# Moments and scales of y for thirteen batches made in the first layer, each kept in a place of its own

## The chip, the cores and the metric

The kernel runs on one core of a Trainium2 chip. The time is device microseconds of one execution. The core has five engines that run their own instruction lists in order and meet through semaphores: TensorE (PE, matrix products), VectorE (DVE), ScalarE (ACT), GpSimd (POOL) and SyncE (SP, which here issues DMA transfers).

## What is computed

`x` is 16 batches of 512 nodes by 128 features, `adj` a 512 by 512 matrix. There are two residual layers, cut here to what matters:

```
h = relu(layernorm(x))
x = x + L0(h)      # eight Euler steps of a graph diffusion
h = relu(layernorm(x))
x = x + L1(h)      # see below

def L1(h):         # softmax attention with 4 heads of 32
    lam_max = eigvalsh(L)[-1]
    L_norm = 2.0 * L / lam_max - I
    z = relu(layernorm((L_norm @ h) @ Wc + bc) * g1 + be1)
    x1 = z + h
    o = masked_attention(x1 @ Wq, x1 @ Wk, x1 @ Wv) @ Wo + bo
    x2 = layernorm(x1 + o) * g2 + be2
    m = gelu(x2 @ W1 + b1) @ W2 + b2
    return layernorm(x2 + m) * g3 + be3
```

The change is about the second `relu(layernorm(x))`. The sum x + L0(h) is called `y` in the kernel; its layer norm needs a mean and a variance for each of the 512 nodes of a batch.

## The kernel before

All data of the 16 batches stay on the chip: `y` holds them as 128 partitions by 16 x 512. A batch is four tiles of 128 nodes.

The program is two blocks, `layer0` and `layer1`. At the end of a block all five engines wait for each other (the rows call it by L598 for the first block), and only then does the second block start.

**First block.** It runs over pairs of batches, `pair(p)` on each engine, p = 0 to 8; a pair enters at p and leaves at p + 1, so that p = 8 only finishes batches 14 and 15. TensorE makes node powers (`first_power`, L843), feature products (`feature_products`, L880) and the products that join them (`pair_product`, L851). VectorE splits results into a high and a low part (`T_lo`, L1263; `Y1_lo`, L1292), adds up the feature products (`C_out`, L1273 to L1276) and adds the last products to y in two halves (`y_out`, L1301). It makes the moments of x for the next batches (`x_moments`). GpSimd turns these into scales for the first layer norm (`scales`, L656 to L666) and puts x and bias into y (`x_and_bias`, L672), which `C_out` waits for. `pair(5)` and `pair(6)` also hold steps of the power iteration for lam_max and the first steps of the second layer (`early`).

**Second block.** Its loop is `round_(r, s, half)`, r = 1 to 18. In a round one batch is attended to, in 16 units `u`: TensorE makes scores (L1882), VectorE masks them (L2062), ScalarE makes exponentials (L2004), TensorE turns them (L1896), ScalarE or VectorE copies them (L1987, L2049), and TensorE multiplies by the values (L1916). Beside it the next batch is convolved (L1954), standardised (`z_out`, `z_moments`, `z_standard`, `norm_z`) and projected, and the one before leaves. The order within a round is a table of numbers by hand (`AT_X1` to `AT_Z2_STD`).

**Moments and scales of y.** `y_moments` is a wait, four statistics instructions (L305), a wait, and four that aggregate them into `mv_a` (L311), on VectorE. `h_scales` is four small operations on GpSimd (L228, L230, L238, L241): variance plus epsilon, its inverse root `rstd_a`, mean times root, and its negative `shift_a`. `normalise` (L250, ScalarE) makes h from y with them. There is one `mv_a`, and two places of `rstd_a` and `shift_a` used in turn; the waits on `scales` and `h_ready` guard them. Batches 0 and 1 are done in pair 5 of the first block, on VectorE around the feature products (`early(p, "y0")`, `early(p, "y1")`), on GpSimd between `x_and_bias(10)` and `scales(12)`. Batch 2 is done in pair 7. Batch r + 2, for 3 to 15, is done in round r of the second block: `y_moments` at unit 9 on VectorE, `h_scales` on GpSimd ahead of `add_bo`.

## Time and profile before

| | |
|---|---|
| three runs, us | 867.37, 867.99, 868.82 |
| median | 867.99 |
| profiled execution, us | 868.01 |
| its span, us | 866.2 |
| PE busy | 818.8 us, 95% |
| DVE busy | 646.5 us, 75% |
| ACT busy | 530.5 us, 61% |
| POOL busy | 310.4 us, 36% |
| first block, from the span's start | to about 395.9 us |

The span is what the profiler saw of the execution; 1.8 us of it lie outside. Shares are over the whole span, which joins two stages: in the first block DVE and ACT are about half busy, in the second both are 80 to 90% busy and more. An engine's idle time is shown in brackets behind the instruction that ended it, with the releaser, as inferred from semaphores. TensorE's clock is given as a share of 2.4 GHz, and is 1.00 or 0.50.

### The profile page before, as it was taken

Reading aid. Unit: us, or ns where it says so; the run is one execution under the profiler, and the core shown is the slowest. Engines: PE = TensorE matmul, PEld = TensorE weight load, DVE = VectorE, ACT = ScalarE, POOL = GpSimd, SP = SyncE. Lnnn points to the kernel's source line nnn. Section 1 sums busy time; section 2 is a strip of 40 time slices with the busy share of each in tenths; the row PEclk is TensorE's granted clock in tenths of the full one; section 3 lists DMA queues with packets and bytes.
Section 4 is the critical chain, followed back from the end, with each engine's and each line's share of the span. In section 5 each row is a group of like instructions: output and inputs, shape, how many; then the busy total and the mean of one; then the engine's idle time right before and its main releaser. Section 6 shows DMA issues by size and latency. Waiting matters only on the chain.

```text
span 866.2 us, 18914 instructions
## 1 busy us (share of the span) xinstructions
PE 818.8 (95%) x6609; PEld 690.4 (80%) x6609; DVE 646.5 (75%) x2146; ACT 530.5 (61%) x1223; POOL 310.4 (36%) x406
## 2 busy tenths in 40 slices
PE   6999999999999999998999999999999999999992
PEld 5778989898989888976777777777777777778982
DVE  5956464645477656536899999999999998987998
ACT  4434243434322422325988888898888888887884
POOL 2011121212122415300445545555554545432654
PEclk9999999999999999998999999999999999999997
DMA  6000010101010100312434455423344444322243
GB/s 133 1 13 13 13 37 13 37 14 37 13 37 13 37 25 26 101 46 76 119 94 108 133 136 135 134 94 96 96 124 135 135 136 133 103 49 63 82 139 97
DMA packets 57514, 65.59 MB, mean 76 GB/s; under 512 B 5574, under 2 KB 32844, under 8 KB 57420
## 3 DMA queue, kind: packets, MB, share of 16 engines
q1 hardware_dynamic: 57120, 64.25, 26.6%
q8 instruction: 53, 0.87, 0.4%
q14 instruction: 41, 0.34, 0.1%
q10 hardware_dynamic: 300, 0.13, 0.1%
HBM read 39.59 MB, written 24.77 MB: 74 GB/s over the span
## 4 chain that ended last, share of the span: by engine, by line
PE 21%; DVE 12%; issue 8%; POOL 8%; ACT 3%; DMA 1%; DVEq 0%; SPq 0%; POOLq 0%
PE bank L1896 6%; PE bank L1954 4%; PE bank L1916 4%; PE bank L1882 3%; DVE prob L2062 2%; PE bank L381 2%; POOL z_norm L353 2%; POOL z_gain L349 2%; POOL x_bo L1834 2%; DVE stats L1666 2%; ACT prob L2004 2%; POOL rstd_b L230 2%; PE bank L385 1%; DVE prob L1661 1%; DVE z L2101 1%
## 5 line engine op out<-in xcount | busy, mean ns | idle before, releaser
L2004 ACT ACTIVATE prob<-prob,low 128x512 f32<-128x512 f32 x256 | 183.7, 718 | 28.2 <-DVE low L2062 25.8
L2062 DVE CUSTOM_DVE_ANT_0 prob<-bank,mask 128x512 f32<-128x512 f32 x256 | 171.0, 682 | 8.5 <-PE bank L1882 6.3
L1896 PE MATMUL bank<-ident,prob 128*128 128x128 f32 x1024 | 158.3, 277 | 1.4 <-ACT probT L1987 1.0
L1896 PEld LDWEIGHTS bank<-ident,prob 128*128 128x128 f32 x1024 | 120.8, 141 | 42.1 <-issue 30.6
L1882 PE MATMUL bank<-k_stack,q_stack 96*128 96x512 f32 x256 | 124.1, 485 | 8.6 <-DVE low L2062 7.3
L1987 ACT ACTIVATE probT<-bank 128x512 f32<-128x512 f32 x176 | 103.1, 586 | 22.9 <-PE bank L1896 21.4
L880 PE MATMUL bank<-B_hi,halves 128*128 128x384 f32 x384 | 106.7, 341 | 3.0 <-DVE C L1276 1.6
L851 PE MATMUL bank<-halves,P3T_hi 128*128 128x256 f32 x512 | 93.9, 285 | 0.9 <-DVE halves L1292 0.5
L851 PEld LDWEIGHTS bank<-halves,P3T_hi 128*128 128x128 f32 x512 | 80.5, 191 | 4.4 <-DVE halves L1292 1.3
L880 PEld LDWEIGHTS bank<-B_hi,halves 128*128 128x128 f32 x384 | 70.6, 189 | 6.4 <-DVE halves L1263 2.7
L851 PE MATMUL bank<-halves,P3T_lo 128*128 128x256 f32 x256 | 72.4, 283 | 0.0
L656 POOL TENSOR_SCALAR var_eps<-mv 128x4 f32<-128x4 f32 x16 | 3.6, 226 | 190.0 <-DVE mv L1216 190.0
L1916 PE MATMUL bank<-probT,v 128*32 128x128 f32 x2048 | 69.2, 276 | 0.0
L2049 DVE COPY probT<-bank 128x512 f32<-128x512 f32 x80 | 55.0, 687 | 16.1 <-PE bank L1896 16.0
L880 PE MATMUL bank<-B_lo,halves 128*128 128x384 f32 x192 | 64.8, 337 | 0.0
L1916 PEld LDWEIGHTS bank<-probT,v 128*32 128x32 f32 x2048 | 52.0, 109 | 15.2 <-ACT probT L1987 8.4
L1882 PEld LDWEIGHTS bank<-k_stack,q_stack 96*128 96x128 f32 x256 | 48.6, 190 | 14.9 <-DVE low L2062 12.6
L1042 ACT ACTIVATE halves<-bank 128x512 fp32r<-128x512 f32 x48 | 28.4, 592 | 49.7 <-PE bank L843 49.7
L1051 ACT ACTIVATE Sq<-bank,trace_inv 128x512 fp32r<-128x512 f32 x36 | 24.7, 686 | 52.2 <-PE bank L835 52.2
L1273 DVE TENSOR_TENSOR y<-bank,y 128x128 f32<-128x128 f32 x64 | 18.5, 288 | 48.9 <-PE bank L880 39.4
L1263 DVE TENSOR_TENSOR halves<-bank,halves 128x512 fp32r<-128x512 f32 x48 | 32.9, 687 | 29.5 <-ACT halves L1042 29.4
L1058 ACT ACTIVATE halves<-C 128x512 fp32r<-128x512 f32 x16 | 10.1, 632 | 66.1 <-DVE C L1276 66.1
(277 smaller groups left out, 1919.4 us busy)
## 6 DMA issues: line engine op xcount, KB each, us to landing
k_stack<-bounce_q SPq DMA_DIRECT2D x48, 256.0 KB, 4.0
q_stack<-bounce_k SPq DMA_DIRECT2D x48, 256.0 KB, 5.5
bounce_q<-k_parts SPq DMA_DIRECT2D x32, 256.0 KB, 2.2
bounce_k<-q_parts SPq DMA_DIRECT2D x32, 256.0 KB, 3.8
x_in<-in_x_dram SPq DMA_DIRECT2D x16, 256.0 KB, 2.8
spread<-inverse_sums SPq DMA_DIRECT2D x64, 64.0 KB, 2.1
out_dram<-probT SPq DMA_DIRECT2D x16, 256.0 KB, 2.4
y_shifted<-y_staging SPq DMA_DIRECT2D x14, 256.0 KB, 2.1
```

The source lines that it names most:

```text
L851: last = pe.matmul(psum[2 + nt // 2][:, nt % 2 * 2 * D:(nt % 2 + 1) * 2 * D], power[:, k, nt * P:(nt + 1) * P], c[:, k, :, :].rearrange("p ...
L880: last = pe.matmul(psum[nt % 2][:, 0:GROUP * D], x[:, nt * P:(nt + 1) * P], c[:, m, :, :].rearrange("p i d -> p (i d)"), start=m == 0 and ...
L1042: act.activation(T_parts[m][0], psum[4 + m][:, :], ACT.Copy).then_inc(T_hi_ready[m], 1)
L1263: dve.tensor_tensor(out=T_parts[m][1], in0=psum[4 + m][:, :], in1=T_parts[m][0].bitcast(F32), op=ALU.subtract).then_inc(T_lo_ready[m], 1)
L1882: pe.matmul(psum[u % 2][:, :], q_stack[s][0:STACKS * HD, head, t * P:(t + 1) * P], k_stack[s][0:STACKS * HD, head, :], start=True, stop=Tr ...
L1896: last = pe.transpose(psum[2 + u % 2][:, mt * P:(mt + 1) * P], prob[u % RING][:, mt * P:(mt + 1) * P], ident[:, :])
L1916: last = pe.matmul(psum[6 + s][rows, t * P:(t + 1) * P], v[s][:, mt, rows], probT[(HEADS * t + head) % TURNED][:, mt, :], start=mt == 0, s ...
L1954: last = pe.matmul(A_BANK[:, :], h_part[:, k, :], L_part[:, k, :], start=k == 0 and n == 0, stop=k == NT - 1 and n == 2)
L1987: act.activation(probT[u % TURNED][:, :, :].rearrange("p t n -> p (t n)"), psum[2 + u % 2][:, :], ACT.Copy).then_inc(copied_act, 1)
L2004: act.activation(prob[u % RING][:, :], prob[u % RING][:, :], ACT.Exp, bias=low[:, u % TURNED:u % TURNED + 1], scale=-1.0, accum_out=row_su ...
L2049: dve.tensor_copy(probT[u % TURNED][:, :, :].rearrange("p t n -> p (t n)"), psum[2 + u % 2][:, :]).then_inc(copied_dve, 1)
L2062: dve.tensor_tensor_reduce(prob[u % RING][:, :], psum[u % 2][:, :], mask[:, u // HEADS, :], 1.0, 3e38, ALU.add, ALU.min, low[:, u % TURNED ...
```

## The change

A table `MOMENTS_AT` says in which pair of the first block the moments and scales of which batches are made: batches 0 and 1 in pair 2, 2 and 3 in pair 3, 4 and 5 in pair 4, 6 and 7 in pair 6, 8 in pair 7, and 9 to 12 in pair 8, the last. Batches 13 to 15 stay in rounds 11 to 13 of the second block. `mv_a`, `rstd_a` and `shift_a` get a place for each of the 16 batches; with that the waits for a free place go, and `h_scales` waits for the scales before it, because the small helpers `ve_a` and `mean_rstd_a` are still shared. The tiles behind them in memory move by 896 bytes. The last stage, which used the four old scale tiles as a ring, uses the first four places of `shift_a`.

```diff
@@ -95,6 +95,7 @@
...
 P3_SPLIT_AT = (1, 3, 5)
+MOMENTS_AT = {2: (0, 1), 3: (2, 3), 4: (4, 5), LAM_PAIR: (6, 7), KEY_PAIR: (8,), PAIRS: (9, 10, 11, 12)}
 SHIFT = 0.45
...
@@ -157,12 +158,12 @@
...
         one.stats = tensor(whole, "stats_a", [P, NT, 6])
-        one.mv = tensor(whole, "mv_a", [P, NT, 2])
+        one.mv = tensor(whole, "mv_a", [P, BATCH, NT, 2])
         one.var_eps = tensor(whole, "ve_a", [P, NT])
-        one.rstd = [tensor(whole, f"rstd_a{i}", [P, NT]) for i in range(2)]
+        rstd_a, shift_a = (tensor(whole, n, [P, BATCH, NT]) for n in ("rstd_a", "shift_a"))
+        one.rstd, one.shift = ([tile[:, b, :] for b in range(BATCH)] for tile in (rstd_a, shift_a))
         one.minus_one = tensor(whole, "minus_one", [P, NT])
         one.mean_rstd = tensor(whole, "mean_rstd_a", [P, NT])
-        one.shift = [tensor(whole, f"shift_a{i}", [P, NT]) for i in range(2)]
         one.h = [tensor(whole, f"h{i}", [P, NT, D]) for i in range(2)]
...
@@ -230,15 +231,15 @@
...
 
-def h_scales(pool, one, b, s):
-
-    inverse_root(pool, b, one.mv, one.mv_ready, one.var_eps, one.rstd[s], one.pool_step, one.h_ready, NT * (b - 1),
+def h_scales(pool, one, b):
+
+    inverse_root(pool, b, one.mv[:, b, :, :], one.mv_ready, one.var_eps, one.rstd[b], one.pool_step, one.scales, 2 * b,
                  one.exponent, one.pool_waited)
     pool.wait_ge(one.pool_step, 2 * b + 2)
-    pool.tensor_tensor(out=one.mean_rstd[:, :], in0=one.mv[:, :, 0], in1=one.rstd[s][:, :],
+    pool.tensor_tensor(out=one.mean_rstd[:, :], in0=one.mv[:, b, :, 0], in1=one.rstd[b],
                        op=ALU.mult).then_inc(one.scales, 1)
     pool.wait_ge(one.scales, 2 * b + 1)
-    pool.tensor_tensor(out=one.shift[s][:, :], in0=one.mean_rstd[:, :], in1=one.minus_one[:, :],
+    pool.tensor_tensor(out=one.shift[b], in0=one.mean_rstd[:, :], in1=one.minus_one[:, :],
                        op=ALU.mult).then_inc(one.scales, 1)
...
@@ -248,7 +249,7 @@
...
     act.activation(one.h[s][:, t, :], one.y[:, bass.ds(b * N + t * D, D)], ACT.Relu,
-                   scale=one.rstd[s][:, t:t + 1], bias=one.shift[s][:, t:t + 1]).then_inc(one.h_ready, 1)
+                   scale=one.rstd[b][:, t:t + 1], bias=one.shift[b][:, t:t + 1]).then_inc(one.h_ready, 1)
 
...
@@ -313,8 +314,8 @@
...
 def y_moments(dve, one, b):
-    moments(dve, b, lambda t: one.y[:, bass.ds(b * N + t * D, D)], one.stats, one.stats_ready, one.mv, one.mv_ready,
-            one.scales, 2 * b, one.dve_waited)
+    moments(dve, b, lambda t: one.y[:, bass.ds(b * N + t * D, D)], one.stats, one.stats_ready,
+            one.mv[:, b, :, :], one.mv_ready, one.scales, 0, one.dve_waited)
 
...
@@ -682,9 +683,6 @@
...
                     x_and_bias(2 * p, 0)
-                    if p == LAM_PAIR - 1:
-                        for b in range(2):
-                            h_scales(pool, one, b, b)
                     if p < LAM_PAIR:
...
@@ -703,6 +701,8 @@
...
                         scales(2 * p + 3, 1)
+                    for done in MOMENTS_AT.get(p, ()):
+                        h_scales(pool, one, done)
                 for mt in range(NT):
...
@@ -715,7 +715,8 @@
...
                     pair(p)
-                h_scales(pool, one, 2, 0)
+                for b in MOMENTS_AT[PAIRS]:
+                    h_scales(pool, one, b)
 
...
@@ -1304,10 +1305,6 @@
...
                     step = (p - LAM_PAIR, at)
-                    if step == (-1, "y0"):
-                        y_moments(dve, one, 0)
-                    if step == (-1, "y1"):
-                        y_moments(dve, one, 1)
                     for i in range(APPLIED + 1):
...
@@ -1382,8 +1379,6 @@
...
                         q_lo_out(dve, one, SQ_BANK, 0)
-                    if step == (1, "y2"):
-                        y_moments(dve, one, 2)
 
...
@@ -1462,6 +1457,8 @@
...
                     early(p, "T_lo2")
+                    for done in MOMENTS_AT.get(p, ()):
+                        y_moments(dve, one, done)
                     early(p, "q")
...
@@ -1474,8 +1471,6 @@
...
                         y_out(p, 1)
-                    early(p, "y2")
-                    early(p, "y0")
                     if enters:
...
@@ -1488,7 +1483,6 @@
...
                         early(p, "z0_std")
-                        early(p, "y1")
                         T_lo(1, b)
...
@@ -1759,7 +1753,7 @@
...
         rstd3 = [row_sums[0][:, i * NT:(i + 1) * NT] for i in range(RING)]
-        shift3 = [*one.rstd, *one.shift]
+        shift3 = one.shift[0:RING]
         y_be3_ready, stats3_ready, mv3_ready, pool3, scales3, z3_std_ready, z3_gain_ready, result_ready = (
...
@@ -1852,8 +1846,8 @@
...
                                            ).then_inc(x2_ready, 1)
-                    if within(r, 0, BATCH - 3):
-                        h_scales(pool, one, r + 2, s)
+                    if within(r, MOMENTS_AT[PAIRS][-1] - 1, BATCH - 3):
+                        h_scales(pool, one, r + 2)
                     if enters:
...
@@ -2074,7 +2068,7 @@
...
                             residual(dve, one, r, s)
-                        if u == AT_Y_MOMENTS and within(r, 0, BATCH - 3):
+                        if u == AT_Y_MOMENTS and within(r, MOMENTS_AT[PAIRS][-1] - 1, BATCH - 3):
                             y_moments(dve, one, r + 2)
...
```

The line numbers of the changed kernel differ by one at first and by up to six further down. Two places follow, on two engines each.

VectorE in pair 5, up to the third low half of batch 11. `stats_a` and `mv_a` are the moments of y for batch 1, `stats` and `mv` those of x for batch 12. Before:

```order
L1318 TENSOR_SCALAR v_scaled<-power_rows,trace_inv 128x4
L1322 TENSOR_TENSOR v_diagonal<-ident,v_scaled 128x512
L1281 TENSOR_TENSOR halves<-C,halves 128x4x128
L1263 TENSOR_TENSOR halves<-bank,halves 128x512
L305 BN_STATS stats_a<-y 128x6 x4
L311 BN_AGGR mv_a<-stats_a 128x2 x4
L1263 TENSOR_TENSOR halves<-bank,halves 128x512
L1210 BN_STATS stats<-x_in 128x6 x4
L1216 BN_AGGR mv<-stats 128x2 x4
L1263 TENSOR_TENSOR halves<-bank,halves 128x512
```

After:

```order
L1315 TENSOR_SCALAR v_scaled<-power_rows,trace_inv 128x4
L1319 TENSOR_TENSOR v_diagonal<-ident,v_scaled 128x512
L1282 TENSOR_TENSOR halves<-C,halves 128x4x128
L1264 TENSOR_TENSOR halves<-bank,halves 128x512 x2
L1211 BN_STATS stats<-x_in 128x6 x4
L1217 BN_AGGR mv<-stats 128x2 x4
L1264 TENSOR_TENSOR halves<-bank,halves 128x512
```

The set of batch 1 is gone from between the first and the second low half; it now stands in pair 2.

GpSimd in pair 5, from behind the add of x and bias for batch 10 (L672, L673 in the changed kernel) on. `ve_a` to `shift_a` are scales of y, `var_eps` to `shift_ln` those of x for batch 12. Before:

```order
L228 TENSOR_SCALAR ve_a<-mv_a 128x4
L230 TENSOR_TENSOR rstd_a<-ve_a,exponent 128x4
L238 TENSOR_TENSOR mean_rstd_a<-mv_a,rstd_a 128x4
L241 TENSOR_TENSOR shift_a<-mean_rstd_a,minus_one 128x4
L228 TENSOR_SCALAR ve_a<-mv_a 128x4
L230 TENSOR_TENSOR rstd_a<-ve_a,exponent 128x4
L238 TENSOR_TENSOR mean_rstd_a<-mv_a,rstd_a 128x4
L241 TENSOR_TENSOR shift_a<-mean_rstd_a,minus_one 128x4
L656 TENSOR_SCALAR var_eps<-mv 128x4
L659 TENSOR_TENSOR rstd<-var_eps,exponent 128x4
L662 TENSOR_TENSOR mean_rstd<-mv,rstd 128x4
L666 TENSOR_SCALAR shift_ln<-mean_rstd 128x4
```

After:

```order
L673 TENSOR_TENSOR y<-x_in,bias 128x512
L657 TENSOR_SCALAR var_eps<-mv 128x4
L660 TENSOR_TENSOR rstd<-var_eps,exponent 128x4
L663 TENSOR_TENSOR mean_rstd<-mv,rstd 128x4
L667 TENSOR_SCALAR shift_ln<-mean_rstd 128x4
L673 TENSOR_TENSOR y<-x_in,bias 128x512
```

The two batches' scales of y that stood ahead of those of x are gone.

GpSimd at the end of the first block: the branch ends the block, and the memset is the first operation of the second. Before:

```order
L672 TENSOR_TENSOR y<-x_in,bias 128x512 x2
L679 TENSOR_TENSOR y_staging<-y,bc_all 128x512 x2
L228 TENSOR_SCALAR ve_a<-mv_a 128x4
L230 TENSOR_TENSOR rstd_a<-ve_a,exponent 128x4
L238 TENSOR_TENSOR mean_rstd_a<-mv_a,rstd_a 128x4
L241 TENSOR_TENSOR shift_a<-mean_rstd_a,minus_one 128x4
L598 UNCONDITIONAL_BRANCH
L1818 UNCONDITIONAL_BRANCH
L1866 MEMSET sums_inv 128x128
```

After (the scales of batches 11 and 12; those of 8, 9 and 10 stand right ahead of them in the same form):

```order
L229 TENSOR_SCALAR ve_a<-mv_a 128x4
L231 TENSOR_TENSOR rstd_a<-ve_a,exponent 128x4
L239 TENSOR_TENSOR mean_rstd_a<-mv_a,rstd_a 128x4
L242 TENSOR_TENSOR shift_a<-mean_rstd_a,minus_one 128x4
L229 TENSOR_SCALAR ve_a<-mv_a 128x4
L231 TENSOR_TENSOR rstd_a<-ve_a,exponent 128x4
L239 TENSOR_TENSOR mean_rstd_a<-mv_a,rstd_a 128x4
L242 TENSOR_TENSOR shift_a<-mean_rstd_a,minus_one 128x4
L599 UNCONDITIONAL_BRANCH
L1812 UNCONDITIONAL_BRANCH
L1860 MEMSET sums_inv 128x128
```

One batch's scales stood there, now five do, the last four of which need moments that VectorE makes in the last pair.

VectorE at the end of the first block, from the last pair's two sums and low halves on. Before:

```order
L1281 TENSOR_TENSOR halves<-C,halves 128x4x128
L1288 TENSOR_TENSOR C<-bank,C 128x512 x2
L1292 TENSOR_TENSOR halves<-C,halves 128x512 x2
L1301 TENSOR_TENSOR y<-bank,y 128x2x256 x2
L598 UNCONDITIONAL_BRANCH
```

After:

```order
L1293 TENSOR_TENSOR halves<-C,halves 128x512 x2
L306 BN_STATS stats_a<-y 128x6 x4
L312 BN_AGGR mv_a<-stats_a 128x2 x4
L306 BN_STATS stats_a<-y 128x6 x4
L312 BN_AGGR mv_a<-stats_a 128x2 x4
L306 BN_STATS stats_a<-y 128x6 x4
L312 BN_AGGR mv_a<-stats_a 128x2 x4
L306 BN_STATS stats_a<-y 128x6 x4
L312 BN_AGGR mv_a<-stats_a 128x2 x4
L1302 TENSOR_TENSOR y<-bank,y 128x2x256 x2
L599 UNCONDITIONAL_BRANCH
```

Four sets of moments now stand between the low halves and the two sums of y.

## Rows read from the trace of the kernel before

**Rows 1.** Stretches: busy us (x instructions) per engine, granted clock, DMA share, GB/s; rounds 13, 14.
```profile
695.50:720.20 24.70, 23.94 (x254) 19.05 (x253) 22.66 (x77) 21.64 (x54) 13.02 (x16) 1.00 0.42 119
720.20:744.90 24.70, 23.95 (x254) 19.03 (x253) 21.57 (x69) 20.62 (x51) 11.40 (x12) 1.00 0.42 119
```

**Rows 2.** Timeline of DVE: start us, us, instruction; round 11, moments of y for batch 13.
```profile
658.57 0.87 DVE L305 BATCH_NORM_STATS2 stats_a<-y 128x6 f32<-128x128 f32 x4
...
659.91 0.69 DVE L2062 CUSTOM_DVE_ANT_0 prob<-bank,mask 128x512 f32<-128x512 f32 x1
```

**Rows 3.** Timeline of DVE: first instruction of rounds 11, 12, 14 and 15.
```profile
645.58 0.24 DVE L2084 RECIPROCAL sums_inv<-row_sums 128x16 f32<-128x16 f32 x1
...
670.74 0.24 DVE L2084 RECIPROCAL sums_inv<-row_sums 128x16 f32<-128x16 f32 x1
...
720.22 0.24 DVE L2084 RECIPROCAL sums_inv<-row_sums 128x16 f32<-128x16 f32 x1
...
744.96 0.24 DVE L2084 RECIPROCAL sums_inv<-row_sums 128x16 f32<-128x16 f32 x1
```

**Rows 4.** Timeline of DVE: the turned-copy wait in round 11, and in round 14.
```profile
661.43 0.69 DVE L2049 COPY probT<-bank 128x512 f32<-128x512 f32 x1 [0.82 <-PE bank L1896]
...
735.65 0.69 DVE L2049 COPY probT<-bank 128x512 f32<-128x512 f32 x1 [1.42 <-PE bank L1896]
```

**Rows 5.** Chain that ended last, in order of time: start us, us, what; round 11.
```profile
659.10 0.70 PE bank L1954 x3
```

**Rows 6.** Timelines of POOL, DVE and PE: pair 5, and PE in pair 4 (250.63).
```profile
283.32 0.23 POOL L228 TENSOR_SCALAR ve_a<-mv_a 128x4 f32<-128x4 f32 x1 [7.47 <-DVE mv_a L311]
...
285.23 0.23 POOL L656 TENSOR_SCALAR var_eps<-mv 128x4 f32<-128x4 f32 x1
...
287.33 1.29 POOL L672 TENSOR_TENSOR y<-x_in,bias 128x512 f32<-128x512 f32 x1
...
283.01 0.66 DVE L1263 TENSOR_TENSOR halves<-bank,halves 128x512 fp32r<-128x512 f32 x1
...
288.66 0.29 DVE L1273 TENSOR_TENSOR y<-bank,y 128x128 f32<-128x128 f32 x1 [2.31 <-POOL y L672]
...
289.40 0.44 PE L880 MATMUL bank<-B_hi,halves 128*128 128x384 f32 x1 [1.25 <-DVE C L1276]
...
250.63 0.44 PE L880 MATMUL bank<-B_hi,halves 128*128 128x384 f32 x1 [0.35 <-DVE C L1276]
```

**Rows 7.** Timeline of DVE: wait before the sum of y's first half, pair 3.
```profile
185.47 0.69 DVE L1301 TENSOR_TENSOR y<-bank,y 128x512 f32<-128x512 f32 x1 [2.47 <-PE bank L851]
```

**Rows 8.** Timelines of DVE, POOL and PE: end of the first layer, start of the second.
```profile
392.03 0.69 DVE L1301 TENSOR_TENSOR y<-bank,y 128x512 f32<-128x512 f32 x1 [3.23 <-PE bank L851]
394.90 0.69 DVE L1301 TENSOR_TENSOR y<-bank,y 128x512 f32<-128x512 f32 x1 [2.19 <-PE bank L851]
...
395.88 0.20 POOL L1866 MEMSET sums_inv<- 128x128 f32 x1 [29.86 <-POOLq L598]
...
395.92 0.70 PE L1882 MATMUL bank<-k_stack,q_stack 96*128 96x512 f32 x2 [1.05 <-PEq L598]
```

**Rows 9.** Timeline of POOL: scales of batch 3 in round 1; a scales step after mean_rstd.
```profile
412.11 0.23 POOL L228 TENSOR_SCALAR ve_a<-mv_a 128x4 f32<-128x4 f32 x1 [14.78 <-DVE mv_a L311]
...
413.81 0.20 POOL L241 TENSOR_TENSOR shift_a<-mean_rstd_a,minus_one 128x4 f32<-128x4 f32 x1
413.97 1.27 POOL L1834 TENSOR_TENSOR x_bo<-x,bc_all 128x512 f32<-128x512 f32 x1
...
287.12 0.24 POOL L666 TENSOR_SCALAR shift_ln<-mean_rstd 128x4 f32<-128x4 f32 x1 [0.20 <-POOL mean_rstd L662]
```

**Rows 10.** Stretch with its granted clock, and the chain at half and at full clock.
```profile
398.70:405.60 6.90, 5.83 (x17) 3.84 (x17) 5.18 (x10) 5.12 (x11) 0.00 (x0) 0.51 0.00 0
...
401.87 2.08 PE bank L381 x2
...
425.90 1.12 PE bank L381 x2
```

## What the change does to the time: the prediction

> **What bounds the kernel now.** I read the profile in five steps. First, the stretches of the attention rounds [rows 1]: TensorE is busy 23.95 of 24.70 us at full clock, and VectorE, the engine that the change relieves, comes close with 22 to 23. Which of the two sets the round cannot be read from two high numbers, so the second step is a comparison that the kernel makes by itself. Round 14 has no moments of y (there is no batch 16), no scales of y on GpSimd and three fewer normalising steps on ScalarE; rounds 1 to 13 have all of them. From the first instruction of round 12 to that of round 14, two rounds with the moments, it takes 720.22 - 670.74 = 49.48 us, 24.74 each; round 14 takes 744.96 - 720.22 = 24.74 us [rows 3]. VectorE's time there went into waiting: before the copy of turned weights it waits 1.42 us for TensorE, where it waited 0.82 in round 11 [rows 4], and TensorE's busy time is the same 23.95. Third, the chain of waits: from the convolution to the middle of the round, and so past the moments at 658.57, it lies on TensorE, group behind group, as at 659.10, while VectorE makes them [rows 5]. So the cycle runs TensorE, then VectorE (z), then GpSimd (normalising z), and the moments of y lie beside its TensorE part.
>
> Fourth, the first layer. TensorE hardly waits there; the one long wait is 1.25 us in pair 5 [rows 6]. Fifth, the border between the layers: all engines meet at the end of the first block, and TensorE stands still for 1.05 us before its first scores, at 395.92 [rows 8]. GpSimd has then been waiting for 29.86 us; the last to arrive is VectorE, whose last sum of y ends at 394.90 + 0.69 = 395.59.
>
> **The attention rounds: nothing.** Ten sets of moments (batches 3 to 12) leave rounds 1 to 10. One set takes VectorE from 658.57 to 659.91, 1.34 us [rows 2], so 13.4 us of its work go, and with them some 1.9 us per batch on GpSimd [rows 9]. By round 14 that is worth 0 per round, and that is my term for rounds 2 to 10. In round 1 no convolution follows, and the chain of waits there lies on ScalarE; GpSimd's scales of batch 3 stand ahead of two adds that nobody waits for. 0 again. The bounds of the term: a loss is excluded, since nothing is added; the gain could be at most 13.4 us.
>
> The Trainium skill (Perfetto Trace Analysis, Identifying the Most-Contended Engine) says that for VectorE occupancy fairly tells how close it is to its limit, and that matmul busy time does not for TensorE. By that rule VectorE, at 92% of the round, would be the engine to relieve. Round 14 speaks against it here; what it would give is the first rival.
>
> **Pair 5: a gain of 1.1 us.** There the moments of batches 0 and 1 go. GpSimd now does the scales of batch 1 only when VectorE has made the moments of y in the midst of its densest pair, and the scales of x for batch 12 and the add of x and bias for batch 11 stand behind them: the chain 283.32, 285.23, 287.33, add done at 288.62, VectorE at 288.66 after a wait of 2.31, TensorE at 289.40 after a wait of 1.25 [rows 6]. Without it the scales of x start when their own moments are there. VectorE's second low half could start as soon as ScalarE's high half is done, at 282.06, instead of at 283.01 [rows 6], and the moments of x behind it would let the scales start some 1.0 us before 285.23, at 284.1 to 284.2. From the scales to the end of the add it takes 287.33 + 1.29 - 285.23 = 3.39, so 287.5; VectorE's sums could then start 1.1 us earlier than at 288.66. Pair 4 shows what remains of such a wait when no moments of y stand in it: 0.35 [rows 6], which gives 0.9. I take 1.1, between 0.9 and the whole 1.25. TensorE stands alone on the path from there on, so this reaches the end of the layer.
>
> **Pairs 2, 3, 4, 6, 7: nothing.** The sets that come in stand behind the third low half, ahead of the sum of y's first half, and VectorE waits there: 2.47 us in pair 3 [rows 7] and as much in pair 4, 0.81 in pair 6, where the scaling of the Laplacian stands ahead. Two sets are 2.7 us, 3.0 with the wait between them (a set's statistics need the one before to be through). So that sum comes 0.2 to 0.5 us later in pairs 2 to 4 and some 2 us later in pair 6. Behind it VectorE waits again for TensorE before the second half's sum, and the products need this y only a pair later. On GpSimd two batches of scales, 4 us, come ahead of the add of x and bias of the next pair, which VectorE needs some 12 us after it runs now; the load of x behind that add has as much room. If this cover were gone, each pair would cost up to 2.7 us.
>
> **The border: a loss of 2.9 us.** In the last pair the moments of batches 9 to 12 stand between VectorE's low halves, done at 392.03 - 3.23 = 388.80 [rows 8], and its last two sums. Four sets back to back take 5.4 to 5.9 us, so they end at 394.2 to 394.7, when the second half is nearly there at 394.90: VectorE arrives 0 to 0.2 us later. GpSimd doesn't. Its scales of these four batches can start only behind the first moments, at 388.8 + 1.4 + 0.2 = 390.4, and they go one after the other. One batch takes 412.11 to 413.97, 1.86 us, when the next instruction needs nothing of it [rows 9]. Here the next batch waits for the last of the four operations. Such a step, behind a small operation of its own engine, starts 0.20 us after the end of that one [rows 9], so a batch takes 413.81 + 0.20 + 0.20 - 412.11 = 2.10. Three of these and 1.9 for the last: 390.4 + 6.3 + 1.9 = 398.6. The engines went on 0.33 us after VectorE's end; so TensorE starts at 398.9 instead of 395.92, 3.0 later. Bounds: 2.2 with 1.86 per batch and a start at 390.2; 3.1 at the other end. I take 2.9. Nothing hides it: every engine waits for GpSimd.
>
> **The clock there: +0.2 us.** For 6.9 us from 398.70 the granted clock was 0.51, the 1.2 GHz level, after TensorE had stood or waited on others for much of the time from 394.9 [rows 10]. The products for k and what stands with them took 2.08 us in it against 1.12 in round 2 at full clock, 0.96 more [rows 10]; three smaller TensorE pieces of the chain behind them add 0.85, so the stretch costs 1.8 us. With the pause grown from 1.05 to some 4 us the slow stretch can lie half under the pause, which saves up to 1.2, or last longer, which costs up to 1. I take 0.2.
> The Trainium skill (TensorE: Matmul & The Clock Gate, Terms) puts the penalty of a throttled time at half of it. For 6.9 us that is 3.4 us, an estimate from the page; by it the ends of this term would be about twice as far. The chain shows less, because ScalarE holds it in between.
>
> **Sum.** The profiled execution took 868.01 us in all with a span of 866.2, which is the median of the runs, 867.99. 868.0 - 1.1 + 2.9 + 0.2 = **870.0 us**. Besides, one round in four (three of rounds 3 to 14) takes 25.15 instead of 24.74 us, as round 11 does [rows 3]; how many do in a run moves both kernels by some 0.4 us each, and the three runs lie 1.45 us apart.
>
> **Rivals.**
> VectorE bounds the rounds after all. For it: 92% of the round. Against it: round 14. It would give up to 870.0 - 13.4 = 856.6, and with only the waits of TensorE on VectorE going (some 0.5 us a round), 865.
> The slow stretch slides under the longer pause. The border still costs 2.9 but 1.2 comes back: 868.0 - 1.1 + 2.9 - 1.0 = 868.8. For it: the pause is now as long as the time that passed from the last matmul, near 394.9, to the start of the slow stretch, 3.8 us. Against it: the stretch need not end earlier for that. GpSimd at 1.86 us a batch goes the same way, 869.1.
> The slow stretch grows. The pause and the thin work behind it add up to 13 us instead of 10; one more piece of slow clock, at 0.2 to 0.3 us of each 1.2 us step where ScalarE holds the chain, costs 1: 871.0. This is slower, and it decides as soon as the clock falls before the pause is over and stays low until ScalarE's steps at 406.
>
> **Chances.** Faster or slower is told apart from no change at 0.2%, 1.7 us, about what a measurement of this kernel resolves. Forecast (869.4 to 870.6) 0.45; longer slow stretch 0.17; shorter slow stretch or quicker scales (868.3 to 869.4) 0.28; rounds faster 0.06; something unseen on either side 0.04. The bound, 869.7, cuts the forecast: slower 0.54, same 0.39, faster 0.07. The likeliest time is 870.0 and the range 868.4 to 871.5 leaves out the rounds' gain and the tails.
>
> **What would show it.** In the profile of the changed kernel: rounds 3 to 14 at 24.74 us, the wait before the turned copy of rounds 3 to 10 at about 1.4; TensorE's wait in pair 5 at 0.0 to 0.35; GpSimd's last scale ending 3 us after VectorE's last sum, and the pause before the first scores near 4 us. Wrong would be the forecast if rounds 3 to 10 shrank, if GpSimd did a batch in under 1.8 us, or if TensorE waited for VectorE in pairs 2 to 7.

## The result, and the profile after

| | before | after |
|---|---|---|
| median, us | 868.03 (10 runs) | 870.75 (10 runs) |
| lowest and highest, us | 866.48, 869.52 | 869.30, 871.34 |
| profiled execution, span, us | 868.01, 866.2 | 871.34, 869.5 |
| VectorE's last sum of y ends, us | 395.59 | 395.08 |
| GpSimd's last scale ends, us | 366 | 397.94 |
| first scores, us | 395.92 | 398.29 |
| first instruction of round 2, us | 422.28 | 425.21 |

The changed kernel is slower: 1.0031 of the time before, 95% interval 1.0021 to 1.0041, or 2.7 us. The forecast was 870.0, 2.0 more than before, with a range of 868.4 to 871.5. The profiled execution of the changed kernel is the longest of its ten, 0.6 us above their median; so what its trace shows adds up to 3.3 us and not to 2.7.

**Pair 5.** The timelines of POOL, DVE and PE of the changed kernel (start us, us, instruction, in brackets the idle time before it and what ended it) answer to [rows 6]:

```profile
284.32 0.23 POOL L657 TENSOR_SCALAR var_eps<-mv 128x4 f32<-128x4 f32 x1 [16.01 <-DVE mv L1217]
...
286.42 1.30 POOL L673 TENSOR_TENSOR y<-x_in,bias 128x512 f32<-128x512 f32 x1
...
287.75 0.29 DVE L1274 TENSOR_TENSOR y<-bank,y 128x128 f32<-128x128 f32 x1 [1.41 <-POOL y L673]
...
288.49 0.45 PE L881 MATMUL bank<-B_hi,halves 128*128 128x384 f32 x1 [0.32 <-DVE C L1277]
```

The scales of x start 0.91 us earlier than at 285.23, VectorE's sum 0.91 earlier than at 288.66, and TensorE waits 0.32 instead of 1.25. The whole first layer is 0.9 us ahead from there on.

**The border.** The same three timelines answer to [rows 8] and [rows 9]; the rows left out on POOL are the other steps of the four batches:

```profile
387.88 0.87 DVE L306 BATCH_NORM_STATS2 stats_a<-y 128x6 f32<-128x128 f32 x4
...
393.53 0.38 DVE L312 BATCH_NORM_AGGREGATE mv_a<-stats_a 128x2 f32<-128x6 f32 x4 [0.50 <-DVE stats_a L306]
393.83 1.25 DVE L1302 TENSOR_TENSOR y<-bank,y 128x512 f32<-128x512 f32 x2
...
389.49 0.23 POOL L229 TENSOR_SCALAR ve_a<-mv_a 128x4 f32<-128x4 f32 x1 [24.55 <-DVE mv_a L312]
...
391.67 0.23 POOL L229 TENSOR_SCALAR ve_a<-mv_a 128x4 f32<-128x4 f32 x1 [0.28 <-POOL shift_a L242]
...
397.74 0.20 POOL L242 TENSOR_TENSOR shift_a<-mean_rstd_a,minus_one 128x4 f32<-128x4 f32 x1
398.25 0.20 POOL L1860 MEMSET sums_inv<- 128x128 f32 x1 [0.32 <-POOLq L599]
...
398.29 0.77 PE L1876 MATMUL bank<-k_stack,q_stack 96*128 96x512 f32 x2 [4.27 <-PEq L599]
```

A batch of scales takes 391.67 - 389.49 = 2.18 us. The last one ends 2.86 us after VectorE's last sum, and TensorE stands still for 4.27 us, where it had been 1.05. From TensorE's start behind its wait in pair 5 to the first scores it was 395.92 - 289.40 = 106.52 us, and is 398.29 - 288.49 = 109.80: 3.28 more.

**The clock behind it.** The stretch at half clock (busy time and instruction count of PE, PEld, DVE, ACT and POOL, then the granted clock) answers to [rows 10]; in the chain that ended last, the products for k still take the slow time:

```profile
398.80:409.00 10.20, 8.63 (x21) 4.95 (x21) 7.93 (x16) 7.04 (x14) 2.19 (x2) 0.50 0.08 30
...
404.24 2.08 PE bank L382 x2
```

It lasts 10.2 us instead of 6.8. From the first scores to the first instruction of round 2 it takes 425.21 - 398.29 = 26.92 us, and took 422.28 - 395.92 = 26.36: 0.56 more.

**The rounds.** VectorE's wait before the turned copy, in round 3, and the stretch of round 7, which have no moments of y any more, answer to [rows 4] and [rows 1]:

```profile
465.19 0.69 DVE L2043 COPY probT<-bank 128x512 f32<-128x512 f32 x1 [1.43 <-PE bank L1890]
...
549.50:574.20 24.70, 23.93 (x254) 19.04 (x253) 21.55 (x69) 21.57 (x54) 11.35 (x12) 1.00 0.44 119
```

VectorE works 1.1 us less in such a round and waits 1.43 us for TensorE; the round stays at 24.74 us. In both kernels a few rounds take some 25.1 us instead, which I call slips. Rounds 2 to 14 together take 748.28 - 425.21 = 323.07 us against 322.68 (the same points of both): 0.39 more, since four rounds take 25.1 instead of three. So the span's +3.3 is -0.91 + 3.28 + 0.56 + 0.39 = 3.32.

### The profile page after: what moved, and what is told of

Read it like the earlier page. It is cut to its first block, busy times and chain, and to the rows that moved or that the text cites. A ratio compares the mean times of both kernels' runs of the same rounds, so it can differ in the third digit from the quotient of the medians.

```text
span 869.5 us, 18915 instructions
## 1 busy us (share of the span) xinstructions
PE 819.8 (94%) x6609; PEld 691.0 (79%) x6609; DVE 647.6 (74%) x2146; ACT 529.9 (61%) x1223; POOL 312.1 (36%) x406
## 4 chain that ended last, share of the span: by engine, by line
PE 20%; DVE 13%; issue 9%; POOL 8%; ACT 4%; DMA 1%; DVEq 0%; SPq 0%; POOLq 0%
PE bank L1890 6%; PE bank L1948 4%; PE bank L1910 3%; PE bank L1876 3%; DVE prob L2056 3%; ACT prob L1998 2%; POOL z_norm L354 2%; POOL z_gain L350 2%; POOL x_bo L1828 2%; PE bank L382 2%; DVE stats L1660 2%; POOL rstd_b L231 2%; PE bank L386 1%; DVE prob L1655 1%; DVE z L2095 1%
## 5 line engine op out<-in xcount | busy, mean ns | idle before, releaser
L1052 ACT ACTIVATE Sq<-bank,trace_inv 128x512 fp32r<-128x512 f32 x36 | 24.8, 688 | 52.2 <-PE bank L836 52.2
L1828 POOL TENSOR_TENSOR x_bo<-x,bc_all 128x512 f32<-128x512 f32 x16 | 20.8, 1300 | 93.0 <-DVE z L2095 91.8
```

The source lines that it names most:

```text
L1828: pool.tensor_tensor(out=x1_bo[s][:, :, :], in0=x1[s][:, :, :], in1=all_tiles(one, BO), op=ALU.add).then_inc(x1_bo_ready, 1)
```

## Experiments

Twelve kernels ran in three groups, each group with the kernel before on its own chip (its medians 867.47, 868.32 and 867.51 us). Times are medians, ratios are to the kernel before of the group, with 95% intervals. One execution differs from the next by 1 us and more, so terms under 1 us are read from the traces, in intervals within a trace.

### Only the scales taken back out of the border

```diff
-                for b in MOMENTS_AT[PAIRS]:
-                    h_scales(pool, one, b)
...
-                    if within(r, MOMENTS_AT[PAIRS][-1] - 1, BATCH - 3):
+                    if within(r, MOMENTS_AT[PAIRS][0] - 2, BATCH - 3):
                         h_scales(pool, one, r + 2)
```

> The changed kernel, but GpSimd's scales of y for batches 9 to 12 are made in rounds 7 to 10 of the second block, as before the change; VectorE's moments of these batches stay in the last pair. Theory (the border is set by GpSimd's serial scales): VectorE's last sum of y ends near 395.1, the scores start near 395.4 instead of 398.29, 2.85 us earlier, and the slow clock stretch shrinks back to some 7 us, 0.5 us more: 870.75 - 3.35 = 867.4 us. Rival 1 (the loss is VectorE's four sets of moments in the last pair, or lies elsewhere in the first block): 870.3 to 870.8, no gain. Rival 2 (the clock's part doesn't depend on the pause): 867.9. Rounds 7 to 10 should stay at 24.74 us with the scales back in them; if GpSimd mattered there they would be longer.

Measured: 867.85 us, ratio 1.0000 (0.9988 to 1.0013). Timelines of DVE and PE:

```profile
394.13 1.25 DVE L1300 TENSOR_TENSOR y<-bank,y 128x512 f32<-128x512 f32 x2
...
395.71 0.70 PE L1874 MATMUL bank<-k_stack,q_stack 96*128 96x512 f32 x2 [1.38 <-PEq L599]
```

VectorE's work is that of the changed kernel, and the scores (L1874) start 0.33 us after its last sum (L1300) ends. From pair 5 (288.84) to the scores it takes 106.87 us, 2.93 less than in the changed kernel and 0.35 more than before. So GpSimd's scales are 2.93 of the 3.28, VectorE's four sets 0.35. Rival 1 falls. The time doesn't tell the theory from rival 2, which differ by 0.5 us. Rounds 7 to 10, with the scales back in them, take 24.76, 25.14, 24.76 and 24.72 us: one slip, as other kernels have them, and nothing else.

### Batches 9 to 12 left in the rounds, and the same once more

```diff
-MOMENTS_AT = {2: (0, 1), 3: (2, 3), 4: (4, 5), LAM_PAIR: (6, 7), KEY_PAIR: (8,), PAIRS: (9, 10, 11, 12)}
+MOMENTS_AT = {2: (0, 1), 3: (2, 3), 4: (4, 5), LAM_PAIR: (6, 7), KEY_PAIR: (8,)}
...
```

(the loop of scales at the end of the first block goes, and the two conditions in the rounds start with batch 9)

> The changed kernel, but both moments and scales of batches 9 to 12 stay in rounds 7 to 10; only batches 0 to 8 are made in the first block. Theory: the border is as in the kernel before (VectorE's end 395.59 - 0.92 = 394.7, scores near 395.0), nothing is lost in the rounds: 870.75 - 3.35 - 0.4 = 867.0, that is 0.9 to 1.0 us under the kernel before, ratio 0.9989. Rival (VectorE's moments cost the rounds in which they stand, some 0.5 us each for four rounds): 869.0. The difference to the run with only the scales taken out prices VectorE's four sets at the border: 0.4 us by the theory, 0 if they are hidden.

> The version with batches 0 to 8 moved and 9 to 15 left in the rounds once more, to narrow its time and to stand beside the other three on one chip. Theory: 0.9 us under the kernel before, ratio 0.9989. Rival (the gain of pair 5 is given back by a longer slow stretch behind the border): ratio 1.0000.

Measured: 866.81 us, 0.9991 (0.9982 to 1.0001); again, 867.42 us, 0.9997 (0.9985 to 1.0010). From pair 5 to the scores 106.51 and 106.61 us, as before the change. The loss at the border is gone in both, and the first run's rival (869.0) falls. Whether the 0.9 us of pair 5 remains in the time is not decided: theory (0.9989) and rival (1.0000) of the second run both lie within its interval.

### Only pair 5 relieved

```diff
+MOMENTS_AT = {2: (0, 1), KEY_PAIR: (2,)}
...
```

(the two places further down follow the table as above)

> Only the sets of batches 0 and 1 are made earlier, in pair 2 instead of pair 5; batch 2 stays in pair 7 and batches 3 to 15 in the rounds, each with a place of its own as in the changed kernel. Theory: the whole gain of the change comes from pair 5, TensorE's wait there falls from 1.25 to 0.32: 868.03 - 0.92 = 867.1. Rival 1 (the wait comes back in pair 6 or at the border): 868.0. Rival 2 (the ten sets taken from rounds 1 to 10 are worth something too): this run would be above the one in which batches 0 to 8 are moved, by more than 0.5 us; by the theory the two agree within 0.4 us.

Measured: 867.44 us, 0.9995 (0.9985 to 1.0005). In its trace TensorE waits 0.34 us in pair 5, from there to the scores it is 106.49 us. Nothing comes back in the first block. The two runs above have six sets fewer in the rounds than this one (batches 3 to 8; the ten of the expectation hold for the changed kernel). The first of them stands 0.6 us under it on the same chip, just past the 0.5 that I had set for rival 2; but each of the two is uncertain by about 0.9, and the second, on a chip of its own, has 0.9997 beside 0.9995. So the times leave rival 2 open here; what speaks against it is in the traces, where the rounds without a slip take 24.74 us in all these kernels, with the sets and without, and the run with more statistics below. The gain of 0.9 is plain in the trace, but the time alone doesn't separate it from none. What it may have met is the clock: the slow stretch behind the border was 10.2 us long here, and there was another in round 16 (below).

### A fifth batch at the border

```diff
-MOMENTS_AT = {2: (0, 1), 3: (2, 3), 4: (4, 5), LAM_PAIR: (6, 7), KEY_PAIR: (8,), PAIRS: (9, 10, 11, 12)}
+MOMENTS_AT = {2: (0, 1), 3: (2, 3), 4: (4, 5), LAM_PAIR: (6, 7), KEY_PAIR: (8,), PAIRS: (9, 10, 11, 12, 13)}
```

> The changed kernel with batch 13 too in the last pair: five sets of moments and scales there instead of four, one fewer in round 11. Theory: GpSimd's chain grows by one batch, 2.19 us, VectorE's end by 1.43 us and stays behind it: scores 2.19 us later, round 11 unchanged: 870.75 + 2.2 = 872.95, plus 0 to 0.4 where the slow clock lasts longer again. Rival 1 (what counts is VectorE's end): +1.4, 872.2. Rival 2 (the slow clock now lies under the pause for a good part): 871.8 to 872.4, with the first products for k of the second block back near 1.1 us.

Measured: 872.86 us, 1.0061 (1.0048 to 1.0074): 5.4 above the kernel before, where the changed one was 2.7. Timelines of DVE and PE:

```profile
395.66 1.25 DVE L1302 TENSOR_TENSOR y<-bank,y 128x512 f32<-128x512 f32 x2
...
400.89 1.19 PE L1876 MATMUL bank<-k_stack,q_stack 96*128 96x512 f32 x2 [6.46 <-PEq L599]
```

TensorE's pause grows by 6.46 - 4.27 = 2.19 us, which is one batch of scales (2.18), though VectorE's last sum comes only 1.3 us later counted from pair 5 (288.99). From there to the scores it is 111.90 us, 2.10 more than in the changed kernel. Rival 1 (VectorE's end) falls. Rival 2 falls by the time; the slow clock did begin in the pause, at 397.4, but lasted 13.6 us.

### Two places for GpSimd's small helpers

```diff
+        one.ve = [one.var_eps, tensor(whole, "ve_a1", [P, NT])]
+        one.mr = [one.mean_rstd, tensor(whole, "mean_rstd_a1", [P, NT])]
...
-    inverse_root(pool, b, one.mv[:, b, :, :], one.mv_ready, one.var_eps, one.rstd[b], one.pool_step, one.scales, 2 * b,
+    inverse_root(pool, b, one.mv[:, b, :, :], one.mv_ready, one.ve[b % 2], one.rstd[b], one.pool_step, one.scales, 2 * b - 2,
...
```

(the two operations behind it use `one.mr[b % 2]` in the same way)

> The changed kernel, but the small helpers ve_a and mean_rstd_a have two places each, used in turn, so that GpSimd starts a batch's scales without waiting for the last step of the batch before. Theory (GpSimd's serial scales set the border): the period per batch falls from 2.18 to some 1.87 us, three times: the last scale ends 0.95 us earlier, scores 0.95 earlier, 870.75 - 0.95 = 869.8, and the step between two batches shows no wait. Rival (something else ends last at the border): the scales get quicker, the scores don't move, 870.75.

Measured: 869.32 us, 1.0018 (1.0009 to 1.0027), 1.0 above the kernel before. Timelines of POOL and PE:

```profile
390.00 0.23 POOL L231 TENSOR_SCALAR ve_a<-mv_a 128x4 f32<-128x4 f32 x1 [24.28 <-DVE mv_a L314]
...
391.71 0.20 POOL L244 TENSOR_TENSOR shift_a<-mean_rstd_a,minus_one 128x4 f32<-128x4 f32 x1
391.92 0.23 POOL L231 TENSOR_SCALAR ve_a<-mv_a 128x4 f32<-128x4 f32 x1
...
398.02 0.70 PE L1878 MATMUL bank<-k_stack,q_stack 96*128 96x512 f32 x2 [3.48 <-PEq L601]
```

The wait of 0.28 between two batches is gone, and the period is 1.92 us. Three steps between four batches are 3 x (2.18 - 1.92) = 0.78 us, and TensorE's pause is 4.27 - 3.48 = 0.79 shorter. From pair 5 (289.17) to the scores it is 108.85 us, 0.95 less than in the changed kernel; that this meets the expected 0.95 is luck, for 0.17 of it lies ahead of GpSimd's first scale (390.00 - 289.17 = 100.83 us against 101.00), which the edit doesn't touch. The scores move with the scales, so the rival falls.

### The same thirteen batches, placed earlier

```diff
-MOMENTS_AT = {2: (0, 1), 3: (2, 3), 4: (4, 5), LAM_PAIR: (6, 7), KEY_PAIR: (8,), PAIRS: (9, 10, 11, 12)}
+MOMENTS_AT = {2: (0, 1), 3: (2, 3), 4: (4, 5), LAM_PAIR: (6, 7), KEY_PAIR: (8, 9, 10), PAIRS: (11, 12)}
```

> The change with the same thirteen batches, placed otherwise: 8, 9 and 10 in pair 7 and only 11 and 12 in pair 8. Theory (the loss is only GpSimd's serial scales behind the last pair's moments): the last scale ends at 389.5 + 4.4 = 393.9, ahead of VectorE's last sum; pause 1.05 us, scores near 395.0: the 3.3 us of the border are gone and the 0.9 of pair 5 stay, 0.9 under the kernel before (ratio 0.9989). Rival (three sets in pair 7 delay the low half of q and the sums of y there): TensorE waits up to 1 us in pair 7, ratio 1.000.

Measured: 866.94 us, 0.9994 (0.9986 to 1.0003). Timelines of POOL, DVE and PE:

```profile
393.68 0.20 POOL L242 TENSOR_TENSOR shift_a<-mean_rstd_a,minus_one 128x4 f32<-128x4 f32 x1
...
394.35 0.69 DVE L1302 TENSOR_TENSOR y<-bank,y 128x512 f32<-128x512 f32 x1 [2.19 <-PE bank L852]
...
395.37 0.70 PE L1876 MATMUL bank<-k_stack,q_stack 96*128 96x512 f32 x2 [1.05 <-PEq L599]
```

The last scale ends before VectorE's last sum starts, the pause is 1.05 us again, and from pair 5 (288.82) to the scores it is 106.55 us. TensorE waits for nothing new in pair 7. All that was meant to move has moved, and the loss is gone. Against the kernel before it is not measurably quicker.

### More statistics in the rounds

The kernel before, with four statistics instructions more per round, on the same y:

```diff
                         if u == AT_Y_MOMENTS and within(r, 0, BATCH - 3):
+                            for t in range(NT):
+                                dve.bn_stats(spare[:, t, :], y[:, bass.ds((r + 2) * N + t * D, D)])
                             y_moments(dve, one, r + 2)
```

> The kernel before with four statistics instructions more (into a tile of their own) ahead of the moments of y in rounds 1 to 13: 0.87 us more on VectorE per round. Theory (VectorE does not bound the rounds; it waits 0.82 us for TensorE before the turned copy behind the moments): that wait falls to about 0, rounds stay at 24.74 or grow by 0.05 to 0.1 us: 0 to +1.3 us against the kernel before. Rival (VectorE bounds the rounds): +0.87 x 13 = +11.3 us. In between (part of the time shows where TensorE waits for masks right behind): +0.3 per round, +4 us, rounds at 25.0.

Measured: 868.40 us, 1.0005 (0.9994 to 1.0016), 0.1 us above the kernel before for 11.3 us more work on VectorE. Timeline of DVE in round 11:

```profile
659.08 0.87 DVE L2080 BATCH_NORM_STATS2 spare<-y 128x6 f32<-128x128 f32 x4
...
661.95 0.69 DVE L2050 COPY probT<-bank 128x512 f32<-128x512 f32 x1
```

The wait before the turned copy, 0.82 in [rows 4], is used up, and the rounds in its trace are 24.74 us, or some 25.1 in five of them. VectorE doesn't bound the rounds, in either direction tried: with one set less per round, which takes 1.34 us, and with 0.87 us more. The upper end of the interval is 1.4 us, so both the rival (11.3) and the case in between (4) fall.

### TensorE kept at work at the border

In the changed kernel, 33 products without use at the end of the first block; and in the version with batches 9 to 15 in the rounds, 8 of them, with two more products ahead of each of the first six units of round 1:

```diff
+                pe.wait_ge(T_lo_ready[0], BATCH)
+                for i in range(33):
+                    pe.matmul(psum[4][:, 0:2 * D], P3T_parts[0][:, i % NT, 0:P], P3T_parts[0][:, 0, 0:2 * D],
+                              start=True, stop=True)
```

> The changed kernel, with 33 products more on TensorE at the end of the first block (256 columns each, result unused, 4 us at full clock), so that TensorE works on through most of the 4.27 us pause. Theory (the slow stretch comes from TensorE's standing still): it begins later or gets shorter, 3.4 to 6.8 us instead of 10.2, and 0.5 to 1.2 us come back: 869.5 to 870.3. Rival 1 (the thin work of round 1 alone brings the slow clock, as in the kernel before with a pause of 1.05 us): the stretch moves back as a whole, no gain, 870.7. Rival 2 (the added products delay the barrier): above 871.

> The version with batches 0 to 8 moved and 9 to 15 left in the rounds, with 8 such products at the end of the first block and two products of 512 columns (result unused) ahead of each of the first six units of round 1, where TensorE waits for masks and exponentials. Theory (idle TensorE in the pause and in the thin work brings the slow clock, which costs 1.2 to 1.8 us there): granted clock 1.00 throughout, the products for k at 1.12 us, scores to the first instruction of round 2 in 25.0 to 25.4 instead of 26.0 to 27.4: 866.8 - 1.2 = 865.6 us. Rival 1: the clock stays full but the added products delay masks and exponentials by as much, 866.8. Rival 2: the clock falls all the same, 867 to 868.

Measured: 870.88 us, 1.0036 (1.0024 to 1.0049), and 867.96 us, 0.9998 (0.9986 to 1.0011): no gain in either. The stretch with its clock, and the timeline of PE, of the first:

```profile
394.00:412.00 18.00, 13.87 (x81) 9.77 (x79) 11.71 (x28) 9.91 (x22) 6.27 (x12) 1.00 0.16 57
...
398.91 0.70 PE L1880 MATMUL bank<-k_stack,q_stack 96*128 96x512 f32 x2 [0.34 <-PEq L599]
...
404.86 1.12 PE L382 MATMUL bank<-x1T,W_k 128*128 128x512 f32 x2 [2.00 <-ACT x1T L377]
```

The slow clock is gone from the border in both traces. The products for k take 1.12 us instead of 2.08, and TensorE has to wait 2.00 us for ScalarE before them, where it waited 0.92. From the scores to round 2 it is 424.91 - 398.91 = 26.00 us; in the second kernel 26.00 too. That is the time of this stretch without slow clock, and the changed kernel's 26.92 is 0.92 above it. It was 26.01 us, without slow clock too, in the second run of the version with batches 9 to 12 left in the rounds, which has no added products; so in these traces those of round 1 neither cost nor save anything there, and the 25.0 to 25.4 that I had expected for the second kernel was wrong. By the 0.92 the first kernel should have gained 0.9 us; its runs don't show it (2.6 us above the kernel before of their chip, the changed kernel 2.7 above), and with intervals of 0.1% on either side this stays open. In the second kernel alone the time outside the span varied, from 1.8 to 3.7 us, where it is 1.8 or 1.9 in every run of all others; its spans are 865.4 us in the mean, 0.8 under those of the kernel before on that chip, so what it gained is partly hidden by that. Why the time outside grew is not shown.

### Four batches in pair 5

```diff
+MOMENTS_AT = {LAM_PAIR: (4, 5), KEY_PAIR: (6, 7, 8)}
...
+                    if p == LAM_PAIR - 1:
+                        for b in range(4):
+                            h_scales(pool, one, b)
```

(and `y_moments` of batch 0 at "y0", of 1 to 3 at "y1")

> The version with batches 0 to 8 in the first block and 9 to 15 in the rounds, but the sets of batches 0 to 3 stand in pair 5: one on VectorE ahead of the feature sums and three between its second and third low half, the scales of all four on GpSimd ahead of those of x for batch 12 (4 and 5 are in pair 6, 6 to 8 in pair 7). Theory (the gain of pair 5 comes from GpSimd's chain scales, add of x and bias, VectorE's sums): the chain is longer than before the change by one batch of scales, 2.19 us, so TensorE waits 1.25 + 2.2 = 3.4 us for VectorE's sums there: 866.8 + 0.92 + 2.2 = 869.9 on that run's scale, about +3.1 against the same version without it. Rival 1 (what counts is VectorE's own work ahead of the low half): TensorE's wait before that half is 2.5 to 3 us longer, and the wait behind stays near 1.25. Rival 2 (the pair has more room than that): +0.9.

Measured: 873.34 us, 1.0065 (1.0053 to 1.0077): 5.9 above the same version without it, not 3.1. Timelines of POOL, DVE and PE:

```profile
284.77 0.23 POOL L229 TENSOR_SCALAR ve_a<-mv_a 128x4 f32<-128x4 f32 x1 [7.44 <-DVE mv_a L312]
...
293.13 1.27 POOL L673 TENSOR_TENSOR y<-x_in,bias 128x512 f32<-128x512 f32 x1
...
294.43 0.29 DVE L1275 TENSOR_TENSOR y<-bank,y 128x128 f32<-128x128 f32 x1 [3.93 <-POOL y L673]
...
288.04 0.44 PE L882 MATMUL bank<-B_hi,halves 128*128 128x384 f32 x1 [1.61 <-DVE halves L1265]
...
295.17 0.44 PE L882 MATMUL bank<-B_hi,halves 128*128 128x384 f32 x1 [1.54 <-DVE C L1278]
```

I had miscounted: three batches of scales stand in the chain instead of one, so two more, 4.38 us. From the scales of batch 1 to the end of the add it takes 294.40 - 284.77 = 9.63 us, and took 288.62 - 283.32 = 5.30 [rows 6]: 4.33 more. So the chain sets the time, as the theory says: VectorE's sum waits 3.93 us for GpSimd's add, and TensorE for the sums. The signs of rival 1 came too, 2.7 us of waits for the low halves and only 1.54 for the sums; those waits lie under the chain, which ends last. Against the version without it, where the 0.91 of the chain is gone as well, that makes 5.2 of the 5.9 us. Besides there was a slow stretch of 3.4 us behind the first of those waits.

### The copy of h after the residual add

```diff
                     pool.wait_ge(one.h_ready, NT * (b + 1))
+                    pool.wait_ge(x1_ready, b)
```

> The same version, and GpSimd's copy that makes the high part of h waits until VectorE's residual add is done, which otherwise both start at the same moment. Theory (a round takes 25.15 instead of 24.74 us whenever GpSimd's copy gets ahead and the residual add takes 1.15 us): the residual add takes 0.69 in every round, no round over 24.8, 2 to 4 slips of 0.4 us go: ratio to the kernel before 0.9975, some 1.2 us under the version without the wait. Rival (the slips move to another pair of instructions): as many rounds of 25.1, ratio 0.9989.

Measured: 867.48 us, 0.9998 (0.9989 to 1.0008), the same as without the wait on that chip (867.42). In its trace no round is over 24.8 us, GpSimd's copy takes 0.61 us and the residual add 0.69. But of the two traces of the same version without the wait the one on this chip has no slip either (the other has two), so the cure is neither shown nor excluded.

## Why the prediction was right

The forecast was 2.0 us more than before, 2.7 were measured, and the terms:

- **Rounds 2 to 10: 0.** Right. They stay at 24.74 us with VectorE waiting 1.43, the figure that round 14 had given (1.42). The run with more statistics confirms it, and with it the first rival falls.
- **Pair 5: -1.1.** The chain was right, the size slightly off: 0.9 in the trace, the bound I had from pair 4. VectorE's low half started at 282.07, as forecast (282.06), but that is 0.94 us earlier and not 1.0; the scales started at 284.32, not at 284.1 to 284.2, and TensorE's wait kept 0.32 as pair 4 had shown (0.35). I should have taken that row instead of going above it. The times confirm it less well: the six runs that have this gain and not the border's loss came out 0.66, 0.03, 0.57, 0.09, 0.03 (later copy) and 0.36 us (products added) below the kernel before of their chip, each uncertain by about 0.9. Where the rest of it goes, if it goes, is open; the clock behind the border and in round 16 is the candidate that the traces show.
- **Pairs 2, 3, 4, 6, 7: 0.** Right. In pair 6 the first sum of y comes at 309.03, which is 1.85 later than the 308.10 of before less the 0.92 gained, as worked out, and TensorE's waits there are the same.
- **The border: +2.9.** Measured 3.28. The mechanism was right in each step: the run without the scales took 2.93 back, the fifth batch added 2.19 to the pause, the quicker batches took 0.79 off it. Mis-sized was the step between two batches: 0.28 us of wait, where I had taken 0.20 from a step inside a batch, so 2.18 instead of 2.10; and VectorE's 0 to 0.2 was 0.35: its fourth set waited 0.50 us for its own statistics, and the first of the two sums, which had run in the gap at 392.03, now stands behind the sets too (L1302, 1.25 us for both), which I had left out.
- **The clock: +0.2.** Measured 0.56, within the ends I gave. The slow stretch grew, from 6.8 to 10.2 us, as the third rival has it; whether the longer pause did that is not shown, since a kernel with the old pause had 10.2 us too (below). And the price was wrong. I had put 1.8 us on the stretch of before, from pieces that were slower in the chain; with full clock this part takes 26.00 us, so the stretch of before cost 0.36 and that of after 0.92 in these two traces (another with 6.8 us took 26.04). The pieces get shorter, and ScalarE's piece in between, which doesn't, takes over. The rule that halves the throttled time, which I had set beside it, gives 5.1 us for the 10.2, an estimate from the page (the Trainium skill, TensorE: Matmul & The Clock Gate, Terms); the trace shows 0.92.
- **Slips.** Three rounds at 25.1 before, four after. Over all fourteen traces it is none to five, so I count this as no part of the change.

The terms that belong to the change for certain, -0.91 and +3.28, make 2.4 us. The rest of the way to 2.7 lies within the interval of the medians (1.8 to 3.6).

## What to carry to other kernels

Work that goes ahead of a barrier is paid by the engine that ends last there, not by the one that was relieved: look which engine idles before the barrier, and whether the moved chain on it starts only when another engine has just finished. Small dependent operations cost their whole serial time, here 2.18 us for four operations on 4 columns; move them where something longer runs beside them, or take away the helper that chains them. And before an engine at 92% is relieved, find a round of the same kernel that lacks the work: here round 14 told the answer beforehand.

## What was unexpected of the hardware

The stretch of slow clock behind the border had very different lengths in kernels that hardly differ there. From the scores to round 2, over all traces with the length of the stretch at 1.2 GHz behind the border:

| slow stretch, us | kernels | scores to round 2, us |
|---|---|---|
| none | products added (two kernels); 9 to 12 in the rounds, again | 26.00, 26.00, 26.01 |
| 3.4 | scales out; placed earlier; more statistics; later copy; four in pair 5 | 26.41, 26.47, 26.25, 26.40, 26.38 |
| 6.8 | before; 9 to 12 in the rounds | 26.36, 26.04 |
| 10.2 | after; only pair 5; two helpers | 26.92, 27.36, 27.36 |
| 13.6 | fifth batch | 26.76 |

The version with 9 to 12 in the rounds, run twice, and that with only pair 5 relieved have the same pause of 1.05 us and the same work around it, and had 6.8, 0 and 10.2 us of it. So not the pause alone decides, and one trace doesn't tell what a pause costs: I had read 0.2 us of difference into a thing that scatters by 1.3. Still, the three traces with a pause of 3.5 us and more and no products added all have 10.2 us or more, and of the nine with 1.05 to 1.4 us only one has; that the longer pause helps it along is likely, not shown. The lines of the run with only pair 5 relieved, stretch and chain:

```profile
397.41:407.65 10.24, 9.19 (x26) 5.78 (x26) 7.15 (x15) 7.37 (x16) 0.00 (x0) 0.50 0.14 51
...
401.49 2.08 PE bank L382 x2
```

A second slow stretch, of 3.4 us in round 16, was there in five of the fourteen traces and made that round 22.0 instead of 20.9 us. A third one lies in the first layer, near 56 us, and it too differs where the code doesn't: in the two runs of the version with 9 to 12 in the rounds and in that with the later copy, which have the same first block, it took 6.8, 3.4 and 0 us, and TensorE started behind its wait in pair 5 at 290.22, 289.08 and 287.66 us. These and the slips are of the size by which runs of one kernel differ, 3 us and more.

Most slips fit a port that two engines can't use together. GpSimd's copy of h and VectorE's residual add start within 0.01 us of each other in nearly every round, and then either the copy takes 0.61 us and the add 1.15, or the copy 1.16 and the add 0.69; both are quick, 0.61 and 0.69, only where the added wait keeps them apart. All 21 rounds of the fourteen traces in which the add takes 1.15 us are slips, of 25.14 us and more. Seven other slips, of 25.07 to 25.11 us, have an add of 0.69 and stay without a cause. The Trainium skill (SBUF — State Buffer, SBUF: two separate sides) says that an operation of VectorE with two inputs in SBUF and one of GpSimd that reads SBUF lock each other out: the one that starts first holds the port for its whole instruction. The four durations agree with that.
